# A decoder layer on one NeuronCore: attention probabilities turned by VectorE blocks and SBUF transfers instead of by TensorE

## The chip, the cores and the metric

The kernel runs on one core of one Trainium2 chip. The metric is the device time of one execution in microseconds (us), the median of several runs. All times of the trace come from one profiled execution.

## What is computed

Three stages follow one another, each with a residual and a layer norm: a state-space mixer with an MLP, an attention over a context with a gated MLP beside it, and a small feed-forward net with quantised weights. The change is in the second and third. Their reference, cut:

```python
B, S, D, J, HEADS, DH = 32, 112, 256, 375, 16, 64      # J: context rows, one key and one value head for all 16
def xattn(x, context, mask, ...):
    xn, cn = layer_norm(x), layer_norm(context)
    q = (xn @ Wq).reshape(b, n, HEADS, DH).transpose(0, 2, 1, 3) * scale
    k, v = split(cn @ Wkv)
    attn = softmax(einsum('bhid,bjd->bhij', q, k) + mask[:, None])
    out = einsum('bhij,bjd->bhid', attn, v).reshape(b, n, HEADS * DH) @ Wout
    val, gate = split(xn @ W1)
    return out + silu(gate) * val @ W2
x = layernorm(x + xattn(x, ctx, mask, ...))
x = layernorm(x + ffn(x, ...))                          # relu(x @ w1 + b1), quantised, @ w2 + b2
```

Everything but the last net's second product is float32.

## The kernel before

The 32 sequences are taken in NG = 8 groups of GB = 4. After the mixer, the function `attention` runs `group(it)` eight times on each engine. A group has STEPS = 28 steps, seven (NP) for each of the four sequences. A step p handles 128 rows of (head pair, token) in two halves e = 0, 1: eight head pairs times 112 tokens are 896 rows, 7 x 128.

What one step does for its 128 rows, by engine, every engine in its own fixed program order:

- TensorE, `scores` (L1485): two products with K = 64 into PSUM banks 0 and 1, 375 columns each. It waits until VectorE has read the banks of the step before.
- VectorE, `highest` (L1867): adds the mask, takes the row maximum, writes to the slot `pr` (four steps deep). Then `divide` of the step before (L1873 reciprocal, L1876 two multiplications of 128 x 375).
- ScalarE, `copies` of the step before the last (L1739), then `exps` (L1745), the exponential with its row sum.
- TensorE, `turn` of two steps back (L1492): six transposes of 128 x 125 by the identity into banks 2 and 3, which `copies` empties into `pT`.
- TensorE, `times_v` three steps back (L1508): only where the step is the fourth or the seventh of its sequence. It multiplies four or three steps' probabilities by the values `va` into bank 4; `heads_out` on ScalarE (L1755) empties it into `OT`.

Beside these, a planned list of pieces (`schedule`, L1065) hands each step further work in two slots X and Y, the same list on all engines: `query` (q projection), `kv` (keys and values of the next sequence), `out` (the output product over `ff` and `OT`, eight parts), `back` (transposes), `gate` and `value` (the gated MLP, eight tiles each), `ftoken`, `up`, `down` (the last net) and `token`. The pieces go through three PSUM banks, the "seats" (`seat`, L1114): `gate` has seat 0, `value` seat 1, `out` and most `kv` seat 2, and all the others the seat of their number modulo 2. TensorE may start a piece only when the piece before it on the same seat has been read out (`vacant`, L1296). Who reads it out: ScalarE for query, ftoken, token, up and out, VectorE for gate, value, back and down. A gate needs first a tanh on ScalarE (L1776), then a product on VectorE (L1927).

VectorE's order within a step is: `highest`, `divide`, a stage of the context's norm (`CONTEXT`, at steps 0, 1 and 4 of seven), a stage of the tokens' norm (`TOKENS`), the pieces of X and Y, a stage of the norm of the attention's result (`RESULT`), a stage of the last norm (`FINAL`). ScalarE's is: `heads_out`, `copies`, `exps`, then its pieces.

The DMA queue of SyncE (SP) issues everything in program order: the mask of three steps ahead (L1371), at step 6 of seven the eight small SBUF to SBUF transfers that bring the turned values to `va` (`values_in`, L1385), at steps 1 to 3 the context, its roots out to HBM (L1389) and back (L1393). `context_norm` stage 2 (L1889) at step 4 waits for these roots; `kv` at step 5 waits for stage 2.

Of the kernel before, what the change touches and what calls it, by code (L numbers as in the profile page):

```python
# [1054 lines left out]
RESULT, TOKENS, TOKENS_FIRST, FINAL = (10, 11, 12), (20, 21, 22), (16, 17, 20), {STEPS - 2: (0,), STEPS - 1: (1, 2)}  # L1055
CONTEXT = (0, 1, 4)
VPARTS = DH // 32 * (ROWS // 32)
# [42 lines left out]

W1_AT = 10
# [81 lines left out]
def attention(nc, ctx0, PS, apart, ident, xm_dram, ctx_dram, ctx_turned, roots_dram, mask_dram, out_dram, w):  # L1183
# [23 lines left out]
    vT = sb("x_vT", [128, JT, ROWS])  # L1207
    va = sb("x_va", [JP, 2, JT, DH])
    mk = sb("x_mk", [ROWS, SLOT, J])
    pr = sb("x_pr", [ROWS, 2 * SLOT, J])  # L1210
# [3 lines left out]
    pT = sb("x_pT", [JP, 2 * 2 * NV, JT, ROWS])  # L1214
    OT = sb("x_OT", [128, 2, GB, KA * S])
# [6 lines left out]
    x2 = sb("f_x2", [S, GB, D])  # L1222
    fs = sb("f_so", [S, GB, D])
# [24 lines left out]
    c_t = count("c_t", GB)  # L1248
    l_rs = count("x_lrs", 16 * GB)
# [18 lines left out]
    h_c = count("h_c", U)  # L1268
    h_o = count("h_o", NB * GB)
    o_c = count("o_c", 2 * GB)  # L1270
    o_s = count("o_s", 2)
    o_ln = count("o_ln", LN)
# [45 lines left out]
    def batch(p):  # L1318

        return p // NP * NB + p % NP // NV  # L1320

# [44 lines left out]
    def sync(sp, mlp):  # L1366
# [12 lines left out]
        def values_in(i, b):  # L1379
            sp.wait_ge(c_t.sem, c_t.value(i, b + 1))  # L1380
            hold(sp, h_o, i, NB * (b - 1))
            for k in range(DH // 32):
                for q in range(ROWS // 32):
                    n = min(32, JP - 32 * q)
                    sp.dma_start(va[32 * q:32 * q + n, b % 2, :, 32 * k:32 * k + 32], vT[32 * k:32 * k + n, :, 32 * q:32 * q + 32]).then_inc(l_va[b % 2].sem, 16)  # L1385
# [12 lines left out]
        def group(it, first=False, last=False):  # L1398
            for p in range(STEPS):
                if p == 12 and not first and not last:  # L1400
# [35 lines left out]
        def result(i):  # L1436
            sp.wait_ge(f_ln.sem, f_ln.value(i, LN))
            sp.dma_start(out_dram[i * GB:(i + 1) * GB, :, :].rearrange("b s d -> s b d"), fs[:, :, :]).then_inc(f_out.sem, 16)
# [24 lines left out]
        group(NG - 1, last=True)  # L1463
        for h in range(2):
            b0 = (NG - 1) * GB + GH * h
            sp.wait_ge(t_fl.sem, t_fl.value(h, HLN))
            sp.dma_start(out_dram[b0:b0 + GH, :, :].rearrange("b s d -> s b d"), fs[:, pair_of(h), :]).then_inc(t_out.sem, 16)
# [7 lines left out]
    def tensor(pe, mlp):  # L1475
        def scores(i, p):
# [5 lines left out]
            hold(pe, h_m, i, 2 * p)  # L1482
            for e in range(2):
                rows = slice(DH * e, DH * e + DH)
                pe.matmul(bank(e)[:, 0:J], qT[rows, b, r * ROWS:(r + 1) * ROWS], kT[rows, b % 2, :], start=True, stop=True).then_inc(h_s.sem, 1)  # L1485

        def turn(i, p):
            for e in range(2):
                pe.wait_ge(h_n.sem, h_n.value(i, 2 * p + e + 1))
                hold(pe, h_c, i, 2 * p + e - 1)  # L1490
                for t in range(JT):
                    last = pe.transpose(bank(2 + e)[0:JP, t * ROWS:(t + 1) * ROWS], pr[:, 2 * (p % SLOT) + e, t * JP:(t + 1) * JP], ident[:, :])  # L1492
                last.then_inc(h_t.sem, 1)

        def times_v(i, p):
# [3 lines left out]
            pe.wait_ge(h_c.sem, h_c.value(i, 2 * p + 2))  # L1499
# [5 lines left out]
            n, k = r % NV + 1, 2 * NV * (batch(p) % 2)  # L1505
            for t in range(JT):
                for e in range(2):
                    last = pe.matmul(bank(4)[DH * e:DH * e + DH, 0:n * ROWS], va[:, b % 2, t, :], pT[:, k + e:k + 2 * n:2, t, :],  # L1508
                                     start=(t == 0), stop=(t == JT - 1))
            last.then_inc(h_o.sem, 1)  # L1510

        def out_part(it, c, n):
# [7 lines left out]
            for m in range(4 * n, 4 * n + 4):  # L1520
                k, at = m % KA, slice(c * 128, (c + 1) * 128)
                lhs, rhs = (w2[:, k, at], ff[:, k, :]) if m < KH else (wo[:, k, at], OT[:, (it - 1) % 2, :, k * S:(k + 1) * S])
                last = pe.matmul(to[:, 0:T], lhs, rhs, start=(m == 0), stop=(m == KA + KH - 1))  # L1523
            if n == 3:
# [15 lines left out]
        def part(it, piece):  # L1540
# [26 lines left out]
            elif kind == "ftoken":  # L1567
                if n == 0:
                    pe.wait_ge(o_ln.sem, o_ln.value(it - 1, LN))
                tokens(it, piece, x2)  # L1570
# [22 lines left out]
        def group(it, first=False, last=False):  # L1593
            for p in range(STEPS):
                if p == 0 and not first:
                    turn(*back(it, p, 2))
# [3 lines left out]
                if p >= 3 or not first:  # L1600
                    times_v(*back(it, p, 3))
                if p >= 2 or (p == 1 and not first):
                    turn(*back(it, p, 2))
# [9 lines left out]
        def end_out(h, c, k0, k1):  # L1613
# [11 lines left out]
            for m in range(k0, k1):  # L1625
                k, at = m % KA, slice(c * 128, (c + 1) * 128)
                lhs, rhs = (w2[:, k, at], half(ff[:, k, :], h)) if m < KH else (wo[:, k, at], OT[:, (NG - 1) % 2, pair_of(h), k * S:(k + 1) * S])
# [4 lines left out]
        def end_back(h):  # L1632
# [3 lines left out]
            else:  # L1636
                pe.wait_ge(t_fx.sem, t_fx.value(0, 1))
# [530 lines left out]
```

## Time and profile before

| | us |
|---|---|
| median of 3 runs | 1850.46 |
| lowest, highest run | 1850.06, 1851.78 |
| span of the profiled execution, first to last instruction | 1848.1 |

| engine | busy, us | share |
|---|---|---|
| TensorE matmul (PE) | 1761.8 | 95% |
| VectorE (DVE) | 1310.7 | 71% |
| ScalarE (ACT) | 918.7 | 50% |
| GpSimd (POOL) | 420.3 | 23% |

The profile shows one execution. PE is a TensorE matmul, PEld its weight load, SPq the queue of SyncE; a TensorE instruction of float32 stands as two records. "Idle before" is an engine's idle time ahead of an instruction, with who released it. The chain of work that ended last is for 86% of the span TensorE. 107 MB go through SyncE's queue, 21.7% of the 16 DMA engines' time.

### The profile page before, as it was taken

To read this page: it belongs to the slowest core of one execution; us is meant where nothing else is said; L and a number is where in the kernel's file an instruction comes from. 1 tells how busy PE (TensorE), PEld (TensorE's weight loads), DVE (VectorE), ACT (ScalarE), POOL (GpSimd) and SP (SyncE) were. 2 spreads that over 40 slices of the span, in tenths; PEclk is the share of its full clock that TensorE was granted. 3 is DMA by queue.
4 is the path that set the end of the run, shared out by engine and by line. 5 is a ranking of instruction groups with operands and counts; after the bars stand their busy time and mean duration, and the time that the engine had idled before them with its cause. 6 is when DMAs were issued, how large, how long until landed. Compare 5 with 4: busy or idle time off the path is not lost.

```text
span 1848.1 us, 27947 instructions
## 1 busy us (share of the span) xinstructions
PE 1761.8 (95%) x9224; PEld 1020.1 (55%) x9224; DVE 1310.7 (71%) x3971; ACT 918.7 (50%) x2262; POOL 420.3 (23%) x569
## 2 busy tenths in 40 slices
PE   4579999999999998999999999999999999999997
PEld 2356676766767544455545554544555554555466
DVE  6878988988976588476667648747747666765744
ACT  3444553553541465456545545645645654654542
POOL 4868677777872001000000000000000000000000
PEclk8689999999999999999999999999999999999999
DMA  4000000000013343232222222323223322232200
GB/s 132 11 11 11 21 21 11 31 21 27 6 39 111 95 138 103 55 79 73 73 67 72 76 71 65 81 57 80 66 64 79 75 70 68 72 82 58 54 19 21
DMA packets 102318, 109.22 MB, mean 59 GB/s; under 512 B 38592, under 2 KB 95872, under 8 KB 101280
## 3 DMA queue, kind: packets, MB, share of 16 engines
q1 hardware_dynamic: 101712, 106.99, 21.7%
q8 instruction: 75, 1.23, 0.3%
q14 instruction: 67, 0.55, 0.1%
q10 hardware_dynamic: 464, 0.46, 0.1%
HBM read 96.92 MB, written 7.42 MB: 56 GB/s over the span
## 4 chain that ended last, share of the span: by engine, by line
PE 86%; DVE 8%; ACT 2%; DMA 2%; issue 1%; POOL 1%; DVEq 0%; POOLq 0%; ACTq 0%
PE ps L1530 20%; PE ps L1485 9%; PE ps L1492 9%; PE ps L1523 9%; PE ps L1508 8%; PE ps L314 5%; PE ps L440 4%; PE ps L387 4%; PE ps L427 4%; PE ps L405 3%; PE ps L1590 2%; DVE m_u L727 2%; PE ps L373 2%; PE ps L1584 1%; PE ps L1628 1%
## 5 line engine op out<-in xcount | busy, mean ns | idle before, releaser
L1867 DVE CUSTOM_DVE_ANT_0 x_pr<-ps,x_mk 128x375 f32<-128x375 f32 x448 | 227.6, 545 | 306.1 <-issue 238.9
L1739 ACT ACTIVATE x_pT<-ps 125x384 f32<-125x384 f32 x448 | 195.5, 489 | 269.8 <-PE ps L1492 269.2
L1745 ACT ACTIVATE x_pr<-x_pr,x_mx 128x375 f32<-128x375 f32 x448 | 268.2, 608 | 30.4 <-DVE x_mx L1867 30.4
L1492 PEld LDWEIGHTS ps<-ident,x_pr 128*125 128x125 f32 x1344 | 164.5, 187 | 130.9 <-issue 95.7
L1492 PE MATMUL ps<-ident,x_pr 128*125 128x128 f32 x1344 | 205.7, 289 | 2.5 <-DVE x_pr L1876 2.5
L1530 PE MATMUL ps<-x_xn,x_w 128*128 128x448 f32 x512 | 205.7, 543 | 2.1 <-DVE x_ff L1927 2.1
L1485 PE MATMUL ps<-x_kT,x_qT 64*128 64x375 f32 x896 | 202.6, 529 | 4.1 <-DVE x_mx L1867 4.1
L1876 DVE TENSOR_SCALAR x_pr<-x_pr,x_rc 128x375 f32<-128x375 f32 x448 | 170.9, 424 | 8.0
L1508 PE MATMUL ps<-x_pT,x_va 125*64 125x512 f32 (+1 forms) x768 | 158.4, 548 | 0.6 <-ACT x_pT L1739 0.6
L314 PE MATMUL ps<-m_xa,w_in 128*128 128x448 f32 x352 | 148.2, 568 | 6.2 <-ACT m_xa L532 6.2
L1485 PEld LDWEIGHTS ps<-x_kT,x_qT 64*128 64x128 f32 x896 | 67.7, 185 | 126.3 <-issue 114.4
L1530 PEld LDWEIGHTS ps<-x_xn,x_w 128*128 128x128 f32 x512 | 93.0, 191 | 74.1 <-issue 69.6
L1755 ACT ACTIVATE x_OT<-ps 128x512 f32<-128x512 f32 x64 | 34.9, 545 | 191.6 <-PE ps L1508 191.6
L440 PE MATMUL ps<-fc,m_gl 128*112 128x256 f32 x512 | 113.3, 379 | 0.0
L1530 PE MATMUL ps<-x_xn,x_wq 128*128 128x448 f32 x256 | 105.0, 542 | 0.0
L314 PEld LDWEIGHTS ps<-m_xa,w_in 128*128 128x128 f32 x352 | 67.4, 198 | 65.2 <-issue 56.4
L1508 PEld LDWEIGHTS ps<-x_pT,x_va 125*64 125x64 f32 x768 | 49.4, 136 | 93.7 <-issue 92.9
L440 PEld LDWEIGHTS ps<-fc,m_gl 128*112 128x112 f32 x512 | 89.4, 177 | 19.8 <-issue 1.1
L387 PE MATMUL ps<-m_Lm,m_R 64*16 64x64 f32 (+6 forms) x1792 | 80.6, 241 | 9.5 <-POOL m_R L1012 9.5
L1745 ACT ACTIVATION_READ_ACCUMULATOR x_pr<-x_pr,x_mx 128x1 f32 x448 | 89.3, 199 | 0.0
L1530 PE MATMUL ps<-f_xn,f_w 128*128 128x448 f32 x224 | 88.8, 539 | 0.0
L1523 PE MATMUL ps<-x_OT,x_wo 128*128 128x448 f32 x224 | 88.8, 539 | 0.0
(195 smaller groups left out, 2867.3 us busy)
## 6 DMA issues: line engine op xcount, KB each, us to landing
x_mk<-in_mask SPq DMA_DIRECT2D x224, 187.5 KB, 2.4
x_cx<-in_context SPq DMA_DIRECT2D x32, 375.0 KB
x_cT<-in_context_turned SPq DMA_DIRECT2D x32, 375.0 KB, 3.3
x_rb<-context_roots SPq DMA_DIRECT2D x32, 187.5 KB, 4.9
m_Rd<-bc_roots SPq DMA_DIRECT2D x8, 448.0 KB, 3.6
x_mixed<-m_x SPq DMA_DIRECT2D x8, 448.0 KB, 4.0
X<-x_mixed SPq DMA_DIRECT2D x8, 448.0 KB, 4.9
m_X<-in_x SPq DMA_DIRECT2D x7, 448.0 KB, 4.0
```

Of the source, the lines that this page charges most:

```text
L314: last = pe.matmul(to, w_in[:, k, n * 128:(n + 1) * 128], xa[:, k, :], start=(k == 0), stop=(k == KD - 1))
L387: last = pe.matmul(bank(2 * (b % 2) + g)[0:rows, at], Rb[part, c, b, j * S:j * S + rows], Lm[part, c, b * NQ + j, :, :], start=(c == 0), s ...
L440: last = pe.matmul(bank(4 + b // 2)[0:S, (b % 2) * D:(b % 2 + 1) * D], gl[:, k, b * S:(b + 1) * S], fc2[:, k, :], start=(k == 0), stop=(k ...
L1485: pe.matmul(bank(e)[:, 0:J], qT[rows, b, r * ROWS:(r + 1) * ROWS], kT[rows, b % 2, :], start=True, stop=True).then_inc(h_s.sem, 1)
L1492: last = pe.transpose(bank(2 + e)[0:JP, t * ROWS:(t + 1) * ROWS], pr[:, 2 * (p % SLOT) + e, t * JP:(t + 1) * JP], ident[:, :])
L1508: last = pe.matmul(bank(4)[DH * e:DH * e + DH, 0:n * ROWS], va[:, b % 2, t, :], pT[:, k + e:k + 2 * n:2, t, :], start=(t == 0), stop=(t == ...
L1523: last = pe.matmul(to[:, 0:T], lhs, rhs, start=(m == 0), stop=(m == KA + KH - 1))
L1530: last = pe.matmul(to[:, 0:T], weights[:, k, at:at + 128], moving[:, k, :], start=(k == 0), stop=(k == KD - 1))
L1739: act.activation(pT[:, 2 * NV * (batch(p) % 2) + 2 * (p % NP % NV) + e, :, :].rearrange("p t s -> p (t s)"), bank(2 + e)[0:JP, 0:JT * ROWS ...
L1745: act.activation(pr[:, k, :], pr[:, k, :], ACT.Exp, scale=-1.0, bias=mx[:, k:k + 1], accum_out=sums[:, k:k + 1]).then_inc(h_e.sem, 1)
L1867: dve.tensor_tensor_reduce(pr[:, k + e, :], bank(e)[:, 0:J], mk[:, p % SLOT, :], -1.0, 3.0e38, ALU.add, ALU.min, mx[:, k + e:k + e + 1]).t ...
L1876: dve.tensor_scalar(pr[:, k + e, :], pr[:, k + e, :], rc[:, k + e:k + e + 1], None, ALU.mult).then_inc(h_n.sem, 1)
```

## The change

The probabilities are no longer turned by TensorE. ScalarE multiplies by the reciprocal (`scaled`, one step back, in place of VectorE), VectorE transposes 32 x 32 blocks within 384 columns (`turn`, two steps back) into `blocks`, and SyncE brings the blocks to their partitions by 16 transfers from SBUF to SBUF for each V product (`turned_across`, three steps back): each of 32 partitions with 3072 contiguous bytes for a batch of four steps, 2304 for one of three. TensorE's `times_v` is five steps back. `turn` on TensorE and `copies` on ScalarE are gone; the scores get four banks (0 to 3) in place of two, so `scores` waits only for `highest` of two steps back. `pT` has one buffer in place of two: transfers of a batch wait until the V product before has ended. The pieces are placed anew. Three result tiles (`so`, `x2`, `fs`) become one, and a wait for the output transfer moves from `down` to `back`. On ScalarE the order in a step is now `exps`, `scaled`, `heads_out`, pieces. The end of the last group is reordered: up and down of the first half stand ahead of the last V product. The values and the probabilities are padded to 384 columns.

```diff
-RESULT, TOKENS, TOKENS_FIRST, FINAL = (10, 11, 12), (20, 21, 22), (16, 17, 20), {...}
+RESULT, TOKENS, TOKENS_FIRST, FINAL = (12, 13, 16), (20, 23, 24), (16, 17, 20), {...}
+LAG = 5
+PARTS = RB * RB
...
-    for c in range(KD):
-        for n in range(4):
-            at[4 * c + n + (1 if c or n >= 2 else 0), "Y"].append(("out", c, n))
+    for n, p in enumerate(OUT_AT):
+        at[p, "Y"].append(("out", n // 4, n % 4))
     for n, s in enumerate("XY"):
-        at[9, s].append(("back", n))
+        at[11, s].append(("back", n))
+        at[17, s].append(("ftoken", n))
+        at[25 + n, "Y"].append(("down", n))
+        at[26, s].append(("token", n))
     for f in range(KH):
-        at[W1_AT + f, "X"].append(("gate", f))
-        at[W1_AT + f, "Y"].append(("value", f))
-    for n, s in enumerate("XY"):
-        at[18, s].append(("ftoken", n))
-        at[24, s].append(("token", n))
-        at[25, s].append(("down", n))
+        at[GATE_AT[f], "X"].append(("gate", f))
+        at[VALUE_AT[f], "Y"].append(("value", f))
     for n in range(KH):
-        at[20 + n // 2, "XY"[n % 2]].append(("up", n))
+        at[UP_AT[n], "Y"].append(("up", n))
+OUT_AT = (0, 3, 5, 6, 7, 8, 9, 10)
+GATE_AT, VALUE_AT = (9, 11, 13, 14, 15, 16, 17, 20), (10, 12, 13, 14, 16, 17, 19, 21)
+UP_AT = (18, 19, 20, 21, 22, 23, 23, 24)
...
+        def turned_across(i, p):
+            if p % NP not in (NV - 1, NP - 1):
+                return
+            n = batch(p)
+            part = JC * BLK * width_of(n)
+            sp.wait_ge(h_t.sem, h_t.value(i, 2 * p + 2))
+            hold(sp, h_o, i, n)
+            for r in range(RB):
+                for q in range(RB):
+                    sp.dma_start(pT[BLK * q:BLK * q + BLK, r * part:(r + 1) * part],
+                                 blocks[n % 2][BLK * r:BLK * r + BLK, q * part:(q + 1) * part]).then_inc(l_pt.sem, 16)
...
                     masks(it, p + 3)
+                if p >= 3 or not first:
+                    turned_across(*back(it, p, 3))
...
-            hold(pe, h_m, i, 2 * p)
+            hold(pe, h_m, i, 2 * p - 2)
-                pe.matmul(bank(e)[:, 0:J], ...)
-        def turn(i, p):
-                for t in range(JT):
-                    last = pe.transpose(bank(2 + e)[0:JP, ...], pr[...], ident[:, :])
+                pe.matmul(bank(2 * (p % 2) + e)[:, 0:J], ...)
...
-            pe.wait_ge(h_c.sem, h_c.value(i, 2 * p + 2))
+            pe.wait_ge(l_pt.sem, l_pt.value(i, 16 * PARTS * (m + 1)))
...
-                if p >= 3 or not first:
-                    times_v(*back(it, p, 3))
-                if p >= 2 or (p == 1 and not first):
-                    turn(*back(it, p, 2))
+                if p >= LAG or not first:
+                    times_v(*back(it, p, LAG))
...
+        def scaled(i, p):
+            k = 2 * (p % SLOT)
+            act.wait_ge(h_r.sem, h_r.value(i, p + 1))
+            for e in range(2):
+                act.activation(pr[:, k + e, 0:J], pr[:, k + e, 0:J], ACT.Copy, scale=rc[:, k + e:k + e + 1]).then_inc(h_n.sem, 1)
...
-            for e in range(2):
-                dve.tensor_scalar(pr[:, k + e, :], pr[:, k + e, :], rc[:, k + e:k + e + 1], None, ALU.mult).then_inc(h_n.sem, 1)
+        def turn(i, p):
+            if r in (0, NV):
+                hold(dve, l_pt, i, 16 * PARTS * (n - 1))
+            for e in range(2):
+                dve.wait_ge(h_n.sem, h_n.value(i, 2 * p + e + 1))
+                dve.transpose(to[:, :, 2 * (r % NV) + e, :], pr[:, 2 * (p % SLOT) + e, :].rearrange("p (c b) -> p c b", b=BLK)).then_inc(h_t.sem, 1)
```

## Rows read from the trace of the kernel before

**Rows 1.** The page, part 1: busy us (share of the span) xinstructions

```profile
PE 1761.8 (95%) x9224; PEld 1020.1 (55%) x9224; DVE 1310.7 (71%) x3971; ACT 918.7 (50%) x2262; POOL 420.3 (23%) x569
```

**Rows 2.** Timeline of SyncE's queue: the same issue in two following groups

```profile
956.13 0.43 SPq L1396 DMA_DIRECT2D X<-x_mixed  x1
...
1105.87 0.60 SPq L1396 DMA_DIRECT2D X<-x_mixed  x1
```

**Rows 3.** Busy us of PE, PEld, DVE, ACT, POOL, then clock, DMA share, GB/s

```profile
956.13:1105.87 149.74, 149.68 (x641) 76.72 (x640) 99.05 (x372) 80.41 (x216) 0.00 (x0) 1.00 0.27 71
```

**Rows 4.** Timeline of TensorE, one step and the next: start, us, instruction

```profile
1151.96 0.90 PE L1485 MATMUL ps<-x_kT,x_qT 64*128 64x375 f32 x4
1152.79 2.79 PE L1508 MATMUL ps<-x_pT,x_va 125*64 125x512 f32 x12
1155.51 0.92 PE L1492 MATMUL ps<-ident,x_pr 128*125 128x128 f32 x6
1156.27 3.17 PE L1530 MATMUL ps<-f_xn,f_w 128*128 128x448 f32 x8
1159.37 0.90 PE L1485 MATMUL ps<-x_kT,x_qT 64*128 64x375 f32 x4
```

**Rows 5.** Timeline of VectorE, parts of several steps

```profile
1145.84 0.62 DVE L1927 SCALAR_TENSOR_TENSOR x_ff<-x_th,ps 128x448 f32<-128x448 f32 x1 [1.06 <-ACT x_th L1776]
1147.59 0.55 DVE L1867 CUSTOM_DVE_ANT_0 x_pr<-ps,x_mk 128x375 f32<-128x375 f32 x1 [0.30 <-PE ps L1485]
...
1148.53 0.16 DVE L1873 RECIPROCAL x_rc<-x_sum 128x2 f32<-128x2 f32 x1
1148.72 0.74 DVE L1876 TENSOR_SCALAR x_pr<-x_pr,x_rc 128x375 f32<-128x375 f32 x2
1149.38 1.00 DVE L1889 TENSOR_TENSOR x_cT<-x_cT,x_rb 128x375 f32<-128x375 f32 x2
...
1155.25 1.40 DVE L1161 BATCH_NORM_STATS2 x_bn<-X 112x6 f32<-112x256 f32 x4
...
1163.40 0.14 DVE L1171 TENSOR_SCALAR x_st<-x_mv 112x4 f32<-112x4 f32 x1
...
1165.56 0.55 DVE L1867 CUSTOM_DVE_ANT_0 x_pr<-ps,x_mk 128x375 f32<-128x375 f32 x1
```

**Rows 6.** The tile of the turned values: ns min/median/max, starts, forms

```profile
L1940 DVE STREAM_TRANSPOSE x_vT<-x_vT x32: 573/573/576, 617.0 to 1751.8; 64x384 f32<-64x384 f32 x32
```

**Rows 7.** Timeline of ScalarE, one step with a gate

```profile
1143.33 0.87 ACT L1739 ACTIVATE x_pT<-ps 125x384 f32<-125x384 f32 x2 [2.21 <-PE ps L1492]
1144.09 0.61 ACT L1745 ACTIVATE x_pr<-x_pr,x_mx 128x375 f32<-128x375 f32 x1
...
1145.27 0.54 ACT L1776 ACTIVATE x_th<-ps 128x448 f32<-128x448 f32 x1
```

**Rows 8.** Timeline of SyncE's queue: how long issues take

```profile
1003.71 5.30 SPq L1385 DMA_DIRECT2D x_va<-x_vT  x8
...
1098.62 0.28 SPq L1389 DMA_DIRECT2D context_roots<-x_st  x1
1098.95 0.33 SPq L1374 DMA_DIRECT2D x_cx<-in_context  x1
...
1101.73 0.35 SPq L1393 DMA_DIRECT2D x_rb<-context_roots  x1
```

**Rows 9.** The page, part 6: DMA issues, KB each, median us to landing

```profile
x_mk<-in_mask SPq DMA_DIRECT2D x224, 187.5 KB, 2.4
...
x_rb<-context_roots SPq DMA_DIRECT2D x32, 187.5 KB, 4.9
```

**Rows 10.** TensorE idle in the first group: two rows of its timeline

```profile
700.14 0.59 PE L1492 MATMUL ps<-ident,x_pr 128*125 128x128 f32 x3 [2.50 <-DVE x_pr L1876]
702.84 3.36 PE L1530 MATMUL ps<-x_xn,x_w 128*128 128x448 f32 x4 [2.11 <-DVE x_ff L1927]
```

**Rows 11.** Busy us and clock by stretch (columns as in group 3), just after

```profile
705.00:710.00 5.00, 5.00 (x17) 2.33 (x16) 3.68 (x11) 2.26 (x8) 0.00 (x0) 0.67 0.18 42
```

More of the change, by code:

```diff
@@ L1248, in attention @@
     c_t = count("c_t", GB)
+    l_pt = count("x_lpt", 16 * PARTS * NB * GB)
     l_rs = count("x_lrs", 16 * GB)
@@ L1271, in attention @@
     o_s = count("o_s", 2)
+    o_ff = count("o_ff", 1)
     o_ln = count("o_ln", LN)
@@ L1320, in batch, with width_of @@
         return p // NP * NB + p % NP // NV
+    def width_of(n):
+        return 2 * (NV if n % 2 == 0 else NP - NV)
     def half(ap, h):
@@ L1399, in group @@
             for p in range(STEPS):
-                if p == 12 and not first and not last:
+                if p == 13 and not first and not last:
                     sp.wait_ge(o_s.sem, o_s.value(it, 0))
@@ L1504, in times_v @@
                 pe.wait_ge(o_c.sem, o_c.value(i, 2 * b + 1))
-            n, k = r % NV + 1, 2 * NV * (batch(p) % 2)
-            for t in range(JT):
+            n = r % NV + 1
+            turned = pT[:, 0:JW * width_of(m)].rearrange("p (r t w b) -> p r t w b", r=RB, t=JC, b=BLK)
+            for t in range(JC):
                 for e in range(2):
-                    last = pe.matmul(bank(4)[DH * e:DH * e + DH, 0:n * ROWS], va[:, b % 2, t, :], pT[:, k + e:k + 2 * n:2, t, :],
-                                     start=(t == 0), stop=(t == JT - 1))
+                    last = pe.matmul(bank(4)[DH * e:DH * e + DH, 0:n * ROWS], va[:, b % 2, t, :], turned[:, :, t, e::2, :].rearrange("p r n b -> p n r b"),
+                                     start=(t == 0), stop=(t == JC - 1))
             last.then_inc(h_o.sem, 1)
@@ L1569, in part @@
                     pe.wait_ge(o_ln.sem, o_ln.value(it - 1, LN))
-                tokens(it, piece, x2)
+                tokens(it, piece, so)
             elif kind == "up":
@@ L1658, in end_up @@
                     pe.wait_ge(h_m.sem, h_m.value(NG - 1, U))
-                if h == 0 and n == 2:
-                    pe.wait_ge(h_c.sem, h_c.value(NG - 1, U))
                 if KH * h + n >= 4:
@@ L1673, in end_down @@
                 for k in range(KH):
-                    last = pe.matmul(bank((4, 7)[h])[0:S, b * D:(b + 1) * D], hq[:, k, at:at + S], fw2q[:, k, :], start=(k == 0), stop=(k == KH - 1))
+                    last = pe.matmul(bank((6, 7)[h])[0:S, b * D:(b + 1) * D], hq[:, k, at:at + S], fw2q[:, k, :], start=(k == 0), stop=(k == KH - 1))
             last.then_inc(t_dn.sem, 1)
@@ L1732, in scalar @@
     def scalar(act, mlp):
-        def copies(i, p):
-            for e in range(2):
-                u = 2 * p + e
-                act.wait_ge(h_t.sem, h_t.value(i, u + 1))
-                if e == 0 and p % NP % NV == 0:
-                    hold(act, h_o, i, batch(p) - 1)
-                act.activation(pT[:, 2 * NV * (batch(p) % 2) + 2 * (p % NP % NV) + e, :, :].rearrange("p t s -> p (t s)"), bank(2 + e)[0:JP, 0:JT * ROWS], ACT.Copy).then_inc(h_c.sem, 1)
         def exps(i, p):
@@ L1803, in group @@
             for p in range(STEPS):
-                if p >= 3 or not first:
-                    heads_out(*back(it, p, 3))
-                if p >= 2 or not first:
-                    copies(*back(it, p, 2))
                 exps(it, p)
+                if p >= 1 or not first:
+                    scaled(*back(it, p, 1))
+                if p >= LAG or not first:
+                    heads_out(*back(it, p, LAG))
                 parts(it, p, "X", first, last)
@@ L1842, in scalar @@
         group(NG - 1, last=True)
-        for p in (STEPS - 2, STEPS - 1):
-            heads_out(NG - 1, p - 1)
-            copies(NG - 1, p)
+        scaled(NG - 1, STEPS - 1)
+        heads_out(NG - 1, STEPS - 4)
+        end_turned(0)
+        end_up(0, 0, KH)
         heads_out(NG - 1, STEPS - 1)
-        end_turned(0)
-        end_up(0, 0, 2)
         for c in range(KD):
             end_out(1, c)
-        end_up(0, 2, KH)
         end_turned(1)
@@ L1925, in part @@
                 if n == 0 and it >= 1:
-                    filled(dve, it, ("out", KD - 1, 3))
+                    dve.wait_ge(o_ff.sem, o_ff.value(it, 0))
                 dve.scalar_tensor_tensor(out=ff[:, n, :], in0=th[:, n % 2, :], scalar=1.0, in1=src[:, 0:T], op0=ALU.add, op1=ALU.mult).then_inc(done, 1)
@@ L1995, in group @@
                     divide(*back(it, p, 1))
+                if p >= 2 or not first:
+                    turn(*back(it, p, 2))
                 b, r = divmod(p, NP)
@@ L2049, in vector @@
             end_norm(1, stage)
-        for h in range(2):
-            end_down(h)
+        end_down(1)
     return sync, tensor, scalar, vector, gpsimd, early_loads, column_means, mean_weights, centred
```

120 lines of the change are left out of this document (59 added, 61 removed).

## The prediction

> **What bounds the kernel now.** I read the busy line of the page first: TensorE is busy 95% of the span, VectorE 71%, ScalarE 50% [rows 1]. An average over stages says little, so the second view is the period of one group: the same SyncE issue returns after 1105.87 - 956.13 = 149.74 us [rows 2], and in that stretch TensorE is busy 149.68 us at the full 2.4 GHz (clock 1.00), VectorE 99.05, ScalarE 80.41 [rows 3]. So in groups 1 to 7 the time is TensorE's instruction list and nothing else. The third view, its timeline, gives the list's prices from start to start: scores 0.83, a V product of four steps 2.72, the six transposes of a step 0.76, two tiles (up, gate or value) 3.10, so 1.55 each [rows 4].
>
> **What the change takes from TensorE.** 28 x 0.76 = 21.3 us a group; up to 24 if the overlap with the next matmul comes off too (0.92 busy against 0.76 spacing). I take 22.5: the list falls to about 127.2 us. If nothing else bound, seven groups would give 158 us.
>
> **What it puts on the others, per step.** VectorE: before, highest 0.94, reciprocal 0.19, two multiplications 0.66 [rows 5]. The multiplications go, two block transposes of 128 x 384 come. The nearest row is the transpose of 64 x 384, 573 ns listed [rows 6]; `highest` is listed at 0.55 and takes 0.47 of spacing, so I take 0.50 each. Bounds: 0.66 (no dearer than the multiplications) and 1.15 (no overlap) for two; taken 1.0. A step costs VectorE 2.13 us, was 1.79: +9.5 a group, about 113 us of its 127 with the gaps between its small instructions. It is no longer an engine with room. ScalarE: two copies from PSUM 0.76 go, two scaled copies within SBUF come; the exponentials beside them have 0.61 listed and the pair takes 1.18 until the tanh [rows 7]. Bounds 0.76 and 1.22, taken 1.0. This alone is small, but it stands ahead of every piece that ScalarE reads out: after `highest` has begun (d), the exponentials end at d + 1.70, the scaled copies at d + 2.70, a tanh at d + 3.23, the gate's product on VectorE (0.62 [rows 5]) at about d + 3.9, the value's, taken as long, at d + 4.7 with the gaps. V product: same columns, taken at 2.72; it now reads runs of 32 columns. No row shows that. Between nothing and a doubling (four sequences x 4.8 = 19 us a group) I take nothing, since the rows' 128-column runs go at the pace of the others.
>
> **Where TensorE now waits.** I walked one steady group through by these prices: TensorE's steps in the new order, VectorE's step begins when scores are there and the step before is done, seats as they are handed over. Four places do not fit:
> - Steps 11 to 16. VectorE has 6 x 2.13 for the steps, gates 1 to 5 and values 1 to 4 (6.2), two `back` (1.4), `kv` (1.25: the transpose of [rows 6] and an addition taken as long, with a gap), the result's statistics (1.40 listed, 1.6 with aggregates), its root 2.16 (1163.40 to 1165.56) and scaling (taken 1.3), and the context's three stages the same way (1.2, 2.16, and 1.00 as listed), all [rows 5]: 31 us. TensorE has 25.5. A gate may start only when the gate before is read, so TensorE follows: 5.5 us from load and 2.5 from the handovers (back 0 and gate 1 share seat 0 in one slot), 8 together.
> - Step 17. `ftoken` 0 waits for the scaling of step 16 (2.1), gate 6 for `ftoken` 0 to be read, behind exponentials and scaled copies (2.8), value 5 for `ftoken` 1 (0.8): 5.7.
> - Steps 19 to 21. Value 6 and up 1, gate 7 and up 2, value 7 and up 3 share a seat back to back; the second waits for VectorE, which comes to the first only behind `kv`, the tokens' statistics or a context stage: 1.2 + 2.9 + 2.4 = 6.5.
> - Steps 26 and 27. Down 1 and token 1 share seat 1 (2.0); query 2 waits for query 0, late because VectorE carries the last norm's statistics into step 27 (1.4): 3.4.
>
> Sum 23.6 us, which is what the transposes gave back. Before, none of this showed, because transposes and copies filled these times and each seat had one piece a step: the wait for the tanh was VectorE's (1.06 [rows 5]), not TensorE's.
>
> **The transfers.** A batch is 16 issues. The eight small ones take 5.30 us, 0.66 each; single ones of the same plain two-dimensional shape 0.33 (125 rows of 3072 bytes) [rows 8]. Bounds for one issue: 0.37 with its gap, and 0.66; I take 0.45, nearer the plain one by shape, more for queueing. Sixteen then take 7.2 us, and the last lands about 2.4 later (the masks' median [rows 9]): 9.6 us from the second transpose. From there TensorE has three steps less 2.1 us: 7.5 to 15, with the stalls above 9 to 17. Late by some tenths at most. SyncE issues 128 x 0.45 = 58 us more a group on top of about 39; no bound. But at step 2 the sixteen stand ahead of the roots: these go out 7.2 us later, come back after 3.1 (1098.62 to 1101.73 [rows 8]) plus 4.9 [rows 9], and in the first and fourth sequence, whose steps are short, stage 2 and then `kv` wait 1.5 to 2.4 us. I count 1.5 us a group, since the other stalls cover part. Masks are asked for three steps ahead; a delay of 7 us stays under that.
>
> The traces show that issuing is not small: 5.30 us for eight transfers of 12 KB [rows 8]. The Trainium skill, page "DMA: Bandwidth & Descriptors", section "Issuing engines are not separate DMA queues", says the time to initiate a DMA is "usually small relative to the DMA itself"; by that page's fit (2.0 us plus bytes over 436 GB/s) a batch of 1.57 MB would be there after an estimated 5.6 us and no V product would ever wait. I go by the row.
>
> The rows price the turn on TensorE at 0.76 us for six [rows 4], plus ScalarE's copies. The Trainium skill, page "VectorE: DVE Perf Modes", section "Rules for kernel authors", sends a 128 x 128 transpose to TensorE if a result in PSUM will do, and leaves 32 x 32 to VectorE. That speaks against the change; by it the work stays where it was and the time is 1850.
>
> **The sum.** Period 127.2 + 23.6 + 1.5 = 152.3 us, +2.6 against 149.7; seven groups +18, less 3 because the last has no tokens and queries. Group 0 (no output pieces, some 123 us) is paced by VectorE, ScalarE and SyncE: of its 22 us of transposes I count 8 as gained (bounds 0 and 15). The end, where the last batch's transfers (9.6 us) run beside the moved up and down tiles (some 8 us): +2. Span 1848.1 + 18 - 3 - 8 + 2 = 1857; the median of the runs is 2.4 above the profiled span: 1860 us.
>
> **The rivals.**
> - The handovers cost half (rival 1). VectorE's transposes or the scaled copies at their lower bounds, or waits that overlap instead of adding. For it: the scores have four banks, so VectorE has more in store. Period 140 to 141: seven groups -64, time about 1780. All gone would be 1690; the load of steps 11 to 16 speaks against that.
> - V waits for its transfers (rival 2, slower). At 0.66 an issue, sixteen take 10.6 us, ready after 13: late wherever three steps less 2.1 us is under 13, which is six of eight batches, by 1 to 4 us, and the roots by 3 more. It decides from about 0.5 us an issue on. +8 to +12 us a group: about 1925. For it: the nearest row by route (SBUF to SBUF, 32 partitions) is 0.66 [rows 8].
> - The clock (rival 3, slower). In group 0 two idle times of 2.50 and 2.11 us in a row were followed by a stretch at clock 0.67, in which records took twice their time [rows 10, 11]; from 702.84, where four records took 3.36 us (eight take 3.17 [rows 4]), two thirds into the stretch of [rows 11], that is 5.5 us or some more at half clock, 2.8 to 3.4 us of work; I take 3.4. The walk has such pairs in steps 16 and 17 and in 20 and 21. Once a group: +24, time 1885.
> - The change does not do what it says: `turn` still on TensorE. The diff removes every call, so no chance.
>
> **How the numbers follow.** Forecast (1830 to 1890) 0.42; rival 1 0.30; rival 2 0.13; rival 3 0.13; nearly all gained 0.02. A measurement of this kernel tells 0.2% (3.7 us) from no change. Of the forecast's 0.42, 0.10 lies faster by more, 0.07 within and 0.25 slower. Faster 0.10 + 0.30 + 0.02 = 0.42; within 0.07; slower 0.25 + 0.26 = 0.51. The range, 1770 to 1930, cuts the outer parts of rivals 1 and 2; it also covers most of the cost bounds (VectorE's transposes -2 to +1 us a group in steps 11 to 16, scaled copies -1.5 to +1).
>
> **What would show it.** Right: no L1492, period about 152 us, VectorE busy near 107 us of it, TensorE idle in front of gates, `ftoken` and ups with the releaser VectorE or ScalarE, hardly ever a DMA in front of V. Rival 1: those waits about 12 us a group. Rival 2: V's matmuls idle behind the transfers, issues of 0.6 us. Rival 3: clock under 1.00 in every group. The prediction is wrong in its sum if the V product's records grow, or if two transposes take far from 1.0 us.

## The result

| | us |
|---|---|
| changed kernel, median of 4 runs | 2092.28 |
| lowest, highest run | 2087.43, 2093.83 |
| kernel before, on the same chip | 1851.12 |
| ratio, 95% interval | 1.1295 [1.1279, 1.1311] |
| span of the profiled execution | 2092.0 |

The change costs 241 us, where 10 were forecast, and lies outside the range of 1770 to 1930. The profile after, from the page: parts 1 and 2 (clock in tenths by slices of the span), then groups of part 5 (busy, mean ns, idle before and its main releaser) and the issues of part 6 (KB each, median us to landing):

```profile
PE 1724.8 (82%) x7880; PEld 908.4 (43%) x7880; DVE 1346.2 (64%) x3972; ACT 974.7 (47%) x2262; POOL 419.4 (20%) x569
...
PEclk8789999999997879989899989999999999899998
...
L1530 PE MATMUL ps<-x_pT,x_va 128*64 128x512 f32 (+1 forms) x768 | 176.6, 600 | 65.5 <-DMA x_pT<-x_blk 65.5
L1892 DVE STREAM_TRANSPOSE x_blk<-x_pr 128x384 f32<-128x384 f32 x448 | 227.8, 547 | 0.0
...
L1905 DVE TENSOR_TENSOR x_cT<-x_cT,x_rb 128x375 f32<-128x375 f32 x64 | 32.0, 541 | 163.9 <-DMA x_rb<-context_roots 163.9
...
x_pT<-x_blk SPq DMA_DIRECT2D x512, 96.0 KB, 2.1
x_mk<-in_mask SPq DMA_DIRECT2D x224, 187.5 KB, 4.5
...
x_rb<-context_roots SPq DMA_DIRECT2D x32, 187.5 KB, 5.3
```

TensorE is busy 1724.8 us, where it was 1761.8 [rows 1], and is idle 18% of the span. The largest new wait for a transfer is in front of stage 2 of the context norm on VectorE (L1905, 163.9 us), for the roots. The wait in front of the V product (L1530) is 65.5. Against [rows 9] the roots land a little later (5.3 us, before 4.9), the masks clearly later (4.5 us, before 2.4).

The period of one group, by the same SyncE issue as in [rows 2], and that stretch's busy times (PE, PEld, DVE, ACT, POOL, then clock):

```profile
1219.12 0.34 SPq L1421 DMA_DIRECT2D X<-x_mixed  x1
...
1396.58 0.34 SPq L1421 DMA_DIRECT2D X<-x_mixed  x1
```

```profile
1219.12:1396.58 177.46, 142.41 (x474) 61.64 (x473) 103.82 (x371) 87.52 (x214) 0.00 (x0) 0.93 0.50 122
```

A group takes 177.46 us against 149.74. TensorE is busy 7.3 us less than in [rows 3] and idle 35.0 us more. Who ended these idle times, TensorE first, then the longest of VectorE, in the same stretch (total us, times, longest):

```profile
PE ps L1614 <- DVE x_cT L1905: 8.7, 2, 4.4
PE ps L1554 <- DVE x_ff L1943: 6.7, 3, 2.6
PE ps L1554 <- DVE x_so L1962: 5.6, 1, 5.6
PE ps L1530 <- DMA x_pT<-x_blk: 4.6, 3, 2.5
PE ps L1554 <- DVE x_ff L1947: 3.4, 2, 2.2
PE ps L1554 <- ACT f_xn L1789: 3.2, 2, 2.6
```

```profile
DVE x_cT L1905 <- DMA x_rb<-context_roots: 19.1, 3, 7.7
```

Three kinds stand here together: handovers of seats (`x_ff`, `f_xn`), waits that come from VectorE standing still for the roots 19.1 us a group (`x_cT`, and `x_so` behind it), and V's own wait for its transfers (`x_pT`, 4.6). One such place in order of time, SyncE's queue first, then VectorE, then TensorE:

```profile
1370.34 10.06 SPq L1409 DMA_DIRECT2D x_pT<-x_blk  x16
1380.44 0.48 SPq L1414 DMA_DIRECT2D context_roots<-x_st  x1
...
1384.20 0.35 SPq L1418 DMA_DIRECT2D x_rb<-context_roots  x1
```

```profile
1369.20 0.16 DVE L77 SCALAR_TENSOR_TENSOR x_st<-x_st 125x3 f32<-125x3 f32 x1
...
1389.64 1.01 DVE L1905 TENSOR_TENSOR x_cT<-x_cT,x_rb 128x375 f32<-128x375 f32 x2 [4.48 <-DMA x_rb<-context_roots]
1390.57 0.68 DVE L1962 TENSOR_TENSOR x_so<-ps,X 112x512 f32<-112x512 f32 x1
```

```profile
1391.30 3.35 PE L1554 MATMUL ps<-x_xn,x_w 128*128 128x448 f32 x4 [5.64 <-DVE x_so L1962]
```

```profile
1391.30:1394.45 3.15, 3.15 (x5) 1.39 (x6) 0.00 (x0) 0.00 (x0) 0.00 (x0) 0.50 0.00 0
```

The roots are ready at 1369.36 (1369.20 + 0.16). In SyncE's program order the sixteen transfers stand ahead of them; these begin at 1370.34 and take 10.06 us. The roots leave at 1380.44, 11.1 us late, and are asked back at 1384.20; stage 2 begins at 1389.64. VectorE has stood 4.48 us, `back`'s addition (L1962) stands behind stage 2, and TensorE stands 5.64 us for it. After that idle time the granted clock is 0.50, which is 1.2 GHz, and four records take 3.35 us where four take 1.77 in the run without crossing, below.

### The profile page after: what moved, and what is told of

It reads as the page before. It is cut to its first block and busy times, and to the rows that moved or that the text cites. A ratio compares the mean times of both kernels' runs of the same rounds, so it can differ in the third digit from the quotient of the medians.

```text
span 2092.0 us, 25897 instructions
## 1 busy us (share of the span) xinstructions
PE 1724.8 (82%) x7880; PEld 908.4 (43%) x7880; DVE 1346.2 (64%) x3972; ACT 974.7 (47%) x2262; POOL 419.4 (20%) x569
## 5 line engine op out<-in xcount | busy, mean ns | idle before, releaser
L1554 PE MATMUL ps<-x_xn,x_w 128*128 128x448 f32 x512 | 255.1, 634 | 89.8 <-DVE x_so L1962 37.6
L1755 ACT ACTIVATE x_pr<-x_pr,x_rc 128x375 f32<-128x375 f32 x448 | 244.2, 592 | 4.1 <-DVE x_rc L1881 4.1
L1530 PE MATMUL ps<-x_pT,x_va 128*64 128x512 f32 (+1 forms) x768 | 176.6, 600 | 65.5 <-DMA x_pT<-x_blk 65.5
L1892 DVE STREAM_TRANSPOSE x_blk<-x_pr 128x384 f32<-128x384 f32 x448 | 227.8, 547 | 0.0
L1905 DVE TENSOR_TENSOR x_cT<-x_cT,x_rb 128x375 f32<-128x375 f32 x64 | 32.0, 541 | 163.9 <-DMA x_rb<-context_roots 163.9
L1554 PE MATMUL ps<-f_xn,f_w 128*128 128x448 f32 x224 | 100.4, 577 | 39.3 <-DVE x_ff L1947 21.0
L1530 PEld LDWEIGHTS ps<-x_pT,x_va 128*64 128x64 f32 x768 | 53.6, 148 | 169.6 <-issue 86.2
L1614 PE MATMUL ps<-x_cT,x_wkv 128*128 128x375 f32 x128 | 63.9, 633 | 62.9 <-DVE x_cT L1905 62.9
L1943 DVE SCALAR_TENSOR_TENSOR x_ff<-x_th,ps 128x448 f32<-128x448 f32 x64 | 39.5, 618 | 106.0 <-ACT x_th L1786 104.9
L1545 PE MATMUL ps<-x_ff,x_w 128*128 128x448 f32 x224 | 90.2, 546 | 0.0
```

The lines of the kernel that those rows point to most:

```text
L1554: last = pe.matmul(to[:, 0:T], weights[:, k, at:at + 128], moving[:, k, :], start=(k == 0), stop=(k == KD - 1))
L1614: last = pe.matmul(to[:, 0:J], wkv[:, k, :], cT[:, k, :], start=(k == 0), stop=(k == KD - 1))
L1755: act.activation(pr[:, k + e, 0:J], pr[:, k + e, 0:J], ACT.Copy, scale=rc[:, k + e:k + e + 1]).then_inc(h_n.sem, 1)
L1892: dve.transpose(to[:, :, 2 * (r % NV) + e, :], pr[:, 2 * (p % SLOT) + e, :].rearrange("p (c b) -> p c b", b=BLK)).then_inc(h_t.sem, 1)
```

## The experiments

The theory after the result: (A) the sixteen issues hold SyncE's in-order queue, and what stands behind them is late, the roots first. The rivals: (B) V waits for its own transfers; (C) it is the bytes; (D) the handovers of seats cost far more than the walk said (the walk is the prediction's way through one group, step by step). All ratios are against the kernel before on the same chip, with 95% intervals.

**Without the crossing.** No transfers; the V product reads the blocks where VectorE left them.

```diff
-                    turned_across(*back(it, p, 3))
-            pe.wait_ge(l_pt.sem, l_pt.value(i, 16 * PARTS * (m + 1)))
+            pe.wait_ge(h_t.sem, h_t.value(i, 2 * p + 2))
-            turned = pT[:, 0:JW * width_of(m)]...
+            turned = blocks[m % 2][:, :]...
-                hold(dve, l_pt, i, 16 * PARTS * (n - 1))
+                hold(dve, h_o, i, n - 1)
```

> The sixteen transfers are left out and the V product reads the blocks where VectorE wrote them (so the probabilities are not turned across partitions). Everything else stays: scaled copies on ScalarE, block transposes on VectorE, five steps back, the new places of the pieces. If the loss comes from the transfers (their issues on SyncE's queue or their bytes), the period of a group falls from 177.5 us to what the walk gave without them, 127.2 + 23.6 = 151 us, and the time to about 1850. If VectorE's load and the handovers of the seats were mis-sized, the time stays above 1950.

Measured 1895.20 us, 1.0249 [1.0227, 1.0271]. Two following groups, busy and clock:

```profile
1121.76:1276.66 154.90, 136.38 (x473) 58.62 (x472) 103.64 (x371) 87.19 (x214) 0.00 (x0) 0.98 0.29 69
1276.66:1430.29 153.63, 136.36 (x473) 58.59 (x472) 103.65 (x371) 87.06 (x214) 0.00 (x0) 0.98 0.29 69
```

So the transfers are 197 of the 241 us, and all the rest of the change costs 45. That is also 45 over the 1850 expected of this run: the sum of the prediction was short here too, by a smaller part. TensorE's waits in the first of these groups, in order of time, the first eight of eleven:

```profile
1131.41 3.27 PE L1551 MATMUL ps<-x_xn,x_w 128*128 128x448 f32 x8 [2.48 <-DVE x_ff L1940]
...
1143.58 4.97 PE L1551 MATMUL ps<-x_xn,x_w 128*128 128x448 f32 x8 [2.77 <-DVE x_ff L1940]
...
1150.56 0.60 PE L1558 MATMUL ps<-ident,x_so 112*128 112x112 f32 x4 [1.18 <-DVE x_so L1187]
1153.77 2.72 PE L1551 MATMUL ps<-x_xn,x_w 128*128 128x448 f32 x4 [2.61 <-ACT f_xn L1786]
...
1157.86 1.77 PE L1551 MATMUL ps<-x_xn,x_w 128*128 128x448 f32 x4 [0.63 <-ACT f_xn L1786]
...
1169.20 1.77 PE L1551 MATMUL ps<-f_xn,f_w 128*128 128x448 f32 x4 [1.16 <-DVE x_ff L1944]
...
1176.09 1.77 PE L1551 MATMUL ps<-f_xn,f_w 128*128 128x448 f32 x4 [2.59 <-DVE x_ff L1940]
...
1182.61 1.77 PE L1551 MATMUL ps<-f_xn,f_w 128*128 128x448 f32 x4 [2.21 <-DVE x_ff L1944]
```

These are the handovers of the walk. The last three are value 6 and up 1, gate 7 and up 2, value 7 and up 3: predicted 1.2, 2.9 and 2.4 us, measured 1.16, 2.59 and 2.21.

**A quarter of the bytes.** The same sixteen issues, each a quarter as wide (the rest of the probabilities is left out).

```diff
-                    sp.dma_start(pT[..., r * part:(r + 1) * part], blocks[n % 2][..., q * part:(q + 1) * part])
+                    sp.dma_start(pT[..., r * part:r * part + part // 4], blocks[n % 2][..., q * part:q * part + part // 4])
```

> The same sixteen issues for each V product, each with a quarter of the bytes (the rest of the turned probabilities is zero from one memset, so the output is not the reference's). Theory, the number of issues costs: an issue stays at 0.5 to 0.63 us, the period over 170 us, the time within 1% of 2092. Rival, the bytes: issues fall towards 0.33 us and the time below 2000.

Measured 2098.18 us, 1.1347 [1.1322, 1.1372], as expected. No faster than the change, so C falls. The issues are as long as before (median listed 591 ns in both).

**The roots first.** The roots' store and load stand ahead of the sixteen issues.

```diff
-                if p >= 3 or not first:
+                late = p % NP == 2 and not (last and p // NP == GB - 1)
+                if (p >= 3 or not first) and not late:
                     turned_across(*back(it, p, 3))
...
                     roots_out(g, n)
+                    roots_in(g, n)
+                    if p >= 3 or not first:
+                        turned_across(*back(it, p, 3))
```

> At step 2 of seven SyncE issues the roots out and back ahead of the sixteen transfers in place of behind them; nothing else moves. Theory: a closed loop through SyncE's queue (16 issues, 8, 16, roots out, landing, back, landing, stage 2 on VectorE, the next batch's blocks), 177.5 / 4 = 44 us a sequence. Then VectorE's wait for the roots (163.9 us) falls under 40 us, the loop shortens by some 8 us a sequence, and the time falls to 1900 to 1960, near the handovers' 151 us a group. Rival, V's wait for its transfers alone sets the pace: the time stays over 2060.

Measured 2119.63 us, 1.1458 [1.1428, 1.1487]. That is the rival's outcome, not the 1900 to 1960 of the theory. The wait for the roots is all but gone (VectorE 10.2 us in the whole run, before the move 163.9), and TensorE's waits between 900 and 1700 us have a new first line:

```profile
PE ps L1532 <- DMA x_pT<-x_blk: 84.1, 19, 7.6
```

In the change that wait is 21.9 us in the same stretch. Whoever stands second in the queue is late. This run alone can't part A from B.

**All issues from GpSimd.** The sixteen transfers move to GpSimd's queue, in the same order, behind the same waits.

> The sixteen transfers are issued from GpSimd's queue, which has nothing to do in this stage; the halving of w2 moves to step 26 of the first group. Theory, SyncE's order is what binds: VectorE's wait for the roots is gone. If an issue there costs no more than SyncE's 0.63 us, the time is 1860 to 1920; at 1 us each a batch needs 16 us and V waits for it, time about 1950 to 2050. Rival, bytes or VectorE: no change from 2092.

Measured 2074.61 us, 1.1224 [1.1205, 1.1243]. The theory's 1860 to 1920 was missed. Sixteen issues take 7.8 us there, 0.50 each. VectorE's wait for the roots between 900 and 1700 us falls from 81.4 to 26.8 us and isn't gone. In the same stretch TensorE now waits 77.2 us for `x_pT` (21.9 in the change), and GpSimd's queue 165.0 us for V products, since `pT` has one buffer. Landing also changed, by part 6 of the page (KB, median us):

```profile
x_pT<-x_blk POOLq DMA_DIRECT2D x512, 96.0 KB, 2.9
...
x_rb<-context_roots SPq DMA_DIRECT2D x32, 187.5 KB, 9.4
```

The roots land after 9.4 us, not 5.3. Moving sixteen issues to another single queue gains only 18 of the 241 us.

**Ghosts: issued, and no reader waits.** The kernel without crossing, and SyncE issues the sixteen transfers (a quarter wide) all the same, into a tile that nobody reads. To the edits above comes, in `turned_across`:

```diff
+            hold(sp, h_o, i, n - 1)
+            hold(sp, l_pt[n % 2], i, 16 * PARTS * (n // 2))
... (in VectorE's turn)
+                hold(dve, l_pt[n % 2], i, 16 * PARTS * (n // 2))
```

The last line keeps VectorE from overwriting blocks that a ghost of two batches before still reads; the trace puts no idle time of VectorE down to it.

> As no_crossing (1895 us: V reads the blocks, untransferred), but SyncE still issues sixteen transfers for each batch, of a quarter of the bytes, into space that nobody reads and that has two halves. V waits for VectorE's blocks only, so only the occupation of SyncE's queue is added (0.63 us x 128 = 81 us a group). Theory, the roots behind these issues are what costs: VectorE waits for the roots again (over 100 us in all) and the time is 1980 to 2060. Rival, V's own wait for its data costs: the time stays near 1895 to 1920.

Measured 2086.16 us, 1.1270 [1.1248, 1.1293]. A group, and VectorE's wait in it:

```profile
1218.84:1396.40 177.56, 146.01 (x474) 63.24 (x472) 103.70 (x371) 87.10 (x214) 0.00 (x0) 0.91 0.31 76
```

```profile
DVE x_cT L1907 <- DMA x_rb<-context_roots: 17.4, 3, 7.2
```

The period is that of the change (177.46) although no V product waits for a transfer. Occupying SyncE's queue costs 191 us over the kernel without crossing, 26 more than the upper end expected, and that is nearly all that the transfers cost (197).

**Ghosts with V's wait.** The V product waits for the ghosts' landing.

```diff
-            pe.wait_ge(h_t.sem, h_t.value(i, 2 * p + 2))
+            pe.wait_ge(l_pt[m % 2].sem, l_pt[m % 2].value(i, 16 * PARTS * (m // 2 + 1)))
```

> As ghost_free, and V also waits until its sixteen ghost transfers have landed; what is left out against the changed kernel is the hold of the single buffer pT (a batch's transfers behind the V product before). If 12.6 us from the blocks to the last landing are too long for three steps: 20 to 60 us above ghost_free. What remains to quarter_bytes (2098 us) is the single buffer: by the short steps in the second half of each sequence some 20 to 60 us; if there is none, the hold costs nothing.

Measured 2084.79 us, 1.1263 [1.1240, 1.1285]: the same as without that wait, where 20 to 60 us more were expected. Beside the roots' wait, V's wait costs nothing more, so B isn't what sets the time of the change. With quarter width and a single buffer (2098.18) it is 13 us more; that is the single buffer's share in this order of the queue.

**Ghosts with the roots first.** The same move as above, but now V doesn't wait for transfers.

> The kernel in which SyncE still issues all sixteen transfers but nothing waits for them (ghost_free, 2086 us), with one thing moved: the roots' store and load of a sequence are issued ahead of the sixteen transfers, not behind them. The same 448 issues stand in the same queue. If SyncE's occupation costs its 191 us through the roots' chain alone (stage 2 on VectorE waits for context_roots to come back), most of it comes back: 1895 to 1945 us, and VectorE's waits for x_rb fall from over 100 us to under 40. If it costs them through the other loads (mask rows, context, V blocks) or through the packets themselves, the time stays at 2050 to 2090.

Measured 1957.63 us, 1.0574 [1.0544, 1.0604]. Of the 191 us, 129 come back: the roots' chain is the larger part of A. 62 us stay, which puts the time 13 us over the upper end of what was expected. One group, and the wait that stands there now:

```profile
1158.74:1318.32 159.58, 140.06 (x473) 59.92 (x472) 103.52 (x371) 86.88 (x214) 0.00 (x0) 0.96 0.32 83
```

```profile
DVE x_pr L1878 <- DMA x_mk<-in_mask: 5.2, 2, 4.9
```

With the roots ahead, the mask rows come late, 5.2 us a group. The period is 4 to 6 us over that without transfers. That fits, though no run took the masks out by themselves; and seven periods of 5.3 us more give only 37 of the 62 us. By the same `X<-x_mixed` issue in group 1 (835.84 against 806.99 without transfers) 29 us are already lost there, most of it in group 0; that part is not taken apart.

Set beside the first run with the roots ahead, this one says more. There V waited for real transfers into a single buffer, and the time was 2119.63; here it doesn't, and it is 1957.63. So V's wait, with the single buffer, costs about 162 us once the roots are out of its way. In the order of the change it is hidden: the two waits run beside each other, and taking off either one alone (the ghosts, or the roots first) gives back next to nothing. Only both together do (135 of the 241 us).

**Half the ghosts.** Eight issues a batch, nobody waits.

```diff
-            for r in range(RB):
+            for r in (0, 1):
```

> ghost_free with eight transfers a batch in place of sixteen, nothing waiting for them. If the cost grows in proportion to the issues from the first on, the time lies in the middle between 1895 (none) and 2086 (sixteen): about 1990 us. If there is slack in the loop through SyncE that hides the first issues, it lies well below the middle: 1900 to 1950 us (the kernel with eight issues on each of two queues took 1926).

Measured 1928.22 us, 1.0415 [1.0385, 1.0445]. Eight issues cost 33 us, the next eight 158. The waits that stand in SyncE's program ahead of a batch (for the blocks, and for a V product) are the same in both, so by themselves they cost at most the 33; the rest comes with the number of issues. VectorE's wait for the roots in one group:

```profile
DVE x_cT L1907 <- DMA x_rb<-context_roots: 3.5, 2, 2.2
```

The loop through the queue has slack for most of the first 5 us of issues; what goes beyond it is paid, with all that follows from it.

**Two queues.** All transfers real, eight from SyncE and eight from GpSimd, each with its own semaphore.

```diff
-            for r in range(RB):
+            for r in (0, 1):
...
+        def turned_across(i, p):        # on GpSimd
+            for r in (2, 3):
+                for q in range(RB):
+                    pool.dma_start(...).then_inc(l_pp.sem, 16)
```

> Correct data, sixteen transfers for each batch, eight from SyncE's queue and eight from GpSimd's at the same time. If the serial issue (10.1 us on SyncE, 7.8 on GpSimd) is the cause, a batch is there 4 to 5 us earlier, the roots go out 5 us earlier, and the time is 1940 to 2000. If the landing or the single buffer sets the pace, it stays over 2040.

Measured 1926.36 us, 1.0421 [1.0393, 1.0449]. The same bytes and the same number of transfers, 166 us less (14 below the range expected). What stands in one row behind another is halved, for the roots and for V's own transfers alike. This run doesn't part the two; with the ghosts, A is shown.

**More seats.** The kernel without crossing, with the scores back in two banks and the two freed banks as further seats for `query`, `ftoken`, `token`, `up`, `down` and `back`, from group 1 on.

```diff
-MISC = (6, 7, 5)
+MISC = (6, 7, 5, 2, 3)
-    return piece[-1] % 2
+    return piece[-1] % 2 + (0 if old else 3)
-            hold(pe, h_m, i, 2 * p - 2)
+            hold(pe, h_m, i, 2 * p)
-                pe.matmul(bank(2 * (p % 2) + e)[:, 0:J], ...)
+                pe.matmul(bank(e)[:, 0:J], ...)
```

> As no_crossing, but the scores have two banks again, and the two banks so freed are seats of their own for query, ftoken, token, up, down and back, so that no piece follows gate or value on a seat within one step. If the handovers cost what the walk gave (steps 17, 19 to 21, 26 and 27 and part of 11 to 16, some 15 of 23.6 us a group), the time falls from 1895 to 1770 to 1800. If VectorE's load alone sets the pace, it stays over 1870.

Measured 1795.13 us, 0.9699 [0.9682, 0.9716], 100 us below the kernel without crossing. One group:

```profile
1085.80:1226.28 140.48, 133.28 (x473) 58.33 (x472) 103.36 (x371) 86.73 (x214) 0.00 (x0) 0.99 0.30 76
```

The seats are worth 14 us a group, where the walk gave some 15 for these places. So these handovers cost 100 us: without them the change would be 56 us faster than the kernel before, with them it is 45 slower, both without the transfers. D is true as a cost, but of the size that the walk had given, and it is not where most of the missing 231 us went.

**Both costs eased, all data real.** Two queues and more seats.

> The change with both of its found costs eased at once: eight transfers from SyncE and eight from GpSimd, and two more PSUM banks as seats for feed-forward and query pieces, all data real. If both costs are separate and add, 1926 less 100 us for the seats gives about 1826 us, 1.3% below the kernel before. If the seats only let TensorE run into the transfers or the roots sooner, 1870 to 1930 us.

Measured 1827.69 us, 0.9872 [0.9849, 0.9895]: the two costs add (1926 less 100), as expected, and this kernel is faster than the change and, by 1.3%, than the kernel before. A group of it, and the two DMA waits in that group, the roots on VectorE and V on TensorE:

```profile
1110.86:1254.16 143.30, 135.11 (x473) 59.08 (x472) 103.55 (x371) 86.84 (x214) 31.28 (x64) 0.98 0.59 151
```

```profile
DVE x_cT L1929 <- DMA x_rb<-context_roots: 3.1, 2, 2.3
```

```profile
PE ps L1551 <- DMA x_pT<-x_blk: 0.5, 1, 0.5
```

**And the roots first in it.**

> split_seats with the roots' store and load issued ahead of SyncE's eight transfers. If what is left of the queue's cost lies in the roots' chain, it takes 10 to 30 us off split_seats. If the eight transfers then come too late for V product, as the sixteen did (wait of TensorE for x_pT 84 us, 2120 us in all), it is 10 us or more above split_seats.

Measured 1857.31 us, 1.0035 [1.0024, 1.0046], 30 us worse than with the roots behind: between 900 and 1700 us TensorE waits 21.9 us for `x_pT`, where it waited 1.7. With eight issues the roots fit behind V's transfers, and V's transfers don't fit behind the roots' round trip.

## Why the prediction was wrong

**The roots behind the sixteen issues: the step that failed.** The prediction named the place, with 7.2 us of delay, and put it into the sum at 1.5 us a group, in two of four sequences. Measured: 11.1 us of delay, VectorE idle 19.1 us in three of four sequences, and a period of 177.5 against 154.3 without transfers (mean of the two groups shown; over five groups 178.3 against 155.4): 23 us a group. Two things were wrong in this term. First, the issue: 0.45 us was taken, the row nearest by shape, between 0.37 and 0.66. Sixteen took 10.06 us, 0.63 each, near the 0.66 of the row nearest by route (SBUF to SBUF, 32 partitions) [rows 8]. Only the excess over the slack is paid, so 40% more issue time can be most of a wait; the half ghosts show that bend. Second, what stands behind the waiting instruction: only `kv` was named. On VectorE's fixed order everything behind stage 2 waits too, `back`'s addition and the next `highest`, and TensorE with it, whose clock then falls (0.50 after the 5.64 us of idle time).

**Rival 2** had the right issue price and the right point ("decides from about 0.5 us"), but put the wait at V and the roots at 3 us more. In the change V's wait adds nothing to that of the roots (2084.79 with it, 2086.16 without), and the roots cost far more: its 1925 was 167 us short. But with the roots ahead V waits 84.1 us between 900 and 1700 us, so what this rival feared was there, beside the other; the forecast's own "late by some tenths at most" for V was too low as well (TensorE waits 4.6 us for `x_pT` in the group shown, and 36.2 between 600 and 863 us, in the first group and the half of the next).

The rule cited from the Trainium skill (page "DMA: Bandwidth & Descriptors", section "Issuing engines are not separate DMA queues"), that the time to initiate is "usually small relative to the DMA itself", doesn't agree with these runs: sixteen issues take 10.06 us and one lands 2.1 us after its issue. The same sentence says that several issuing engines save only that time, and here that saving is 166 us. The fit on that page, by which the prediction estimated 5.6 us for a batch, is given there (section "Anatomy of one DMA — SWDGE (gpsimd) path") for one DMA issued from GpSimd; here a batch took 10.06 us of issues and 2.1 more to the last landing.

**TensorE's list.** Taken: 22.5 us less a group. Measured: busy 149.68 falls to 136.4 at clock 0.98 and 133.3 at 0.99, so 13 to 16 less. Part of the gap is the clock: busy time multiplied by the clock is an estimated 134 and 132 us of work, 16 to 18 less. Another part is what stands ahead of the tiles: two tiles behind scores took 3.21 us from start to start in the kernel with more seats (1141.33 to 1144.54), where two behind transposes took 3.10 [rows 4], at most an estimated 3 us in 28 steps. Why was not looked into. The rest stays open.

```profile
1141.33 3.27 PE L1551 MATMUL ps<-f_xn,f_w 128*128 128x448 f32 x8
1144.54 0.90 PE L1510 MATMUL ps<-x_kT,x_qT 64*128 64x375 f32 x4
```

**The walk.** It gave 8, 5.7, 6.5 and 3.4 us for its four places. Without crossing the same places hold about 6.3, 4.4, 6.0 and 1.8 (the eight rows above, and behind them 1.01 and 0.81 in steps 26 and 27 and 1.04 in the next group's steps 11 to 13), together 18.5, not 23.6. This error and the one before it have opposite signs, and the period came out 154.3 against 150.8 predicted (152.3 less the 1.5 for the roots). That agreement is partly luck; that the handovers cost what they did is not, as the seats show.

**VectorE and ScalarE.** Two block transposes take 1.02 us, predicted 1.0. VectorE is busy 103.8 us a group, predicted about 107. Two scaled copies take 0.99 us from start to next start (1249.56 to 1250.55), predicted 1.0. V's strided reads cost nothing: 12 records in 2.80 us, before 2.79 [rows 4].

**The clock (rival 3)** came true as well, on top: 0.98 a group without transfers and 0.93 in the change, where before had 1.00 [rows 3]. Busy time multiplied by one minus the clock gives an estimated 2.7 us a group without transfers (the rival said 3.4) and 10 in the change. In the change it follows the long idle times, as at 1391.30.

**Group 0 and the end.** Predicted: 8 us gained and 2 lost. The `X<-x_mixed` in step 13 of group 1 came at 806.39 before, at 806.99 without crossing and at 863.21 in the change. Without crossing, less 2 us for those 13 steps, about 2 us are gained in group 0, not 8. In the change 56 us are lost up to there, of which 11 are group 1's share of 23: so the queue costs some 45 us in group 0 alone, which the prediction had priced at nothing. From the last such issue (1583.93 against 1555.12) to the end it is 309 us without crossing and 293 before; with 7 for the one and a half groups in it, the end costs about 9 us, not 2.

**The rule on transposes** (Trainium skill, page "VectorE: DVE Perf Modes", section "Rules for kernel authors") sends a 128 x 128 transpose to TensorE where a result in PSUM will do. The change as it was built fits it (12.95% slower). The kernel with two queues and more seats doesn't: with TensorE as the bound, the crossing spread over two queues and the free banks used, it turns on VectorE and is 1.3% faster.

## What to carry to other kernels

Price a burst of DMA issues as time on an in-order queue, by the row of the same route, and walk every other load behind it to its reader and to what stands behind that reader on its engine; the loop with the least slack pays, and it pays for the excess only, so ask where the slack ends. A transfer that its own reader hardly waits for can be the most expensive one in the kernel. Where two waits run beside each other, taking off one shows nothing of what the other costs: take off both once. When an engine is relieved of filler work, list which buffers (here PSUM banks as seats) were handed over under its cover, and spend the banks that come free on those.

## What the runs showed of the hardware

- A plain transfer of 32 partitions from SBUF to SBUF holds SyncE's queue for 0.63 us, whether it carries 96 KB or 24 KB (median listed 591 ns in both). In the change the medians listed for others are 0.34 us for `X`, 0.35 for the roots' load, 0.38 for the context, 0.43 for the masks and 0.48 for the roots' store. It lands after 2.1 (96 KB) and 1.8 us (24 KB).
- From GpSimd the same issue takes 0.50 us. With all sixteen there it lands after 2.9 (96 KB) or 3.6 us (72 KB), and the roots' landing on the other queue went from 5.3 to 9.4 us beside it. With eight on each queue the 96 KB ones land after 4.0 us from SyncE and 3.7 from GpSimd, and the roots after 5.0. Why was not looked into.
- After an idle time of 5.64 us of TensorE the clock was 0.50 for the next 3.15 us.
